# Scores for the maxima as three float32r products of split keys, one slot later, in a 32-batch perceiver kernel

## The reference

```
q = _split_heads(query @ Wq.T + bq)          # 64 rows, 16 heads of 16
k = _split_heads(bank @ Wk.T + bk)           # 1601 rows
v = _split_heads(bank @ Wv.T + bv)
scores = jnp.einsum('bhqd,bhkd->bhqk', q / score_scale, k)
attn = jax.nn.softmax(scores, axis=-1)
ctx = jnp.einsum('bhqk,bhkd->bhqd', attn, v)
```

## Time and profile before

| | before |
|---|---|
| time, median of 3 runs | 2134.21 us |
| lowest and highest run | 2132.24, 2140.06 us |
| span of the profiled execution | 2136.6 us |
| PE busy | 1977.4 us (93%) |
| DVE busy | 1327.4 us (62%) |
| ACT busy | 1050.5 us (49%) |
| POOL busy | 616.4 us (29%) |
| mean granted PE clock | 0.982 of 2.4 GHz |

### The profile page before, as it was taken

How to read it: one execution, slowest core, us unless ns; L and a number is a source line. 1 busy time by engine, 2 the same in 40 slices (tenths; PEclk the granted TensorE clock), 3 DMA queues, 4 the chain that set the end, 5 groups by cost and what they waited for, 6 DMA issues and landing times.

```text
span 2136.6 us, 72531 instructions
## 1 busy us (share of the span) xinstructions
PE 1977.4 (93%) x31780; PEld 1592.0 (75%) x31796; DVE 1327.4 (62%) x2500; ACT 1050.5 (49%) x1532; POOL 616.4 (29%) x998
## 2 busy tenths in 40 slices
PE   6789989999999999999999999999999998999987
PEld 4677777777877777787778777777777776777764
DVE  2656656856756666666666576675666666666644
ACT  3354445555465555455554544555545444444442
POOL 3223322323233232333323233342323222122201
PEclk7999999999999999999999999999999999999999
DMA  5433433343432333434333423343342321222122
GB/s 177 164 127 117 158 108 113 121 142 122 147 113 82 123 137 123 151 104 146 105 108 127 150 77 128 106 153 107 113 149 80 117 77 45 92 85 82 49 71 69
DMA packets 98358, 243.89 MB, mean 114 GB/s; under 512 B 12416, under 2 KB 18688, under 8 KB 98048
## 3 DMA queue, kind: packets, MB, share of 16 engines
q1 hardware_dynamic: 97456, 239.22, 32.7%
q10 hardware_dynamic: 592, 0.04, 0.0%
HBM read 235.94 MB, written 3.15 MB: 112 GB/s over the span
## 4 chain that ended last, share of the span: by engine, by line
PE 73%; DVE 13%; ACT 7%; issue 6%; POOL 1%; DMA 0%; ACTq 0%; DVEq 0%; POOLq 0%
PE M L798 11%; PE M L805 11%; PE SC L1016 9%; PE SC L1039 8%; PE O L1060 7%; PE X L855 5%; DVE mx L1607 4%; ACT probT L1262 4%; PE SC L1032 3%; PE M L855 3%; PE X L1126 2%; PE M L899 1%; PE X L1100 1%; PE M L860 1%; PE X L834 1%
## 5 line engine op out<-in xcount | busy, mean ns | idle before, releaser
L1607 DVE TENSOR_REDUCE mx<-SC 128x4 f32<-128x1600 f32 (+1 forms) x256 | 466.7, 1823 | 137.7 <-PE SC L1016 134.3
L1262 ACT ACTIVATE probT<-SC 128x2048 f32<-128x2048 f32 (+1 forms) x256 | 398.8, 1558 | 170.4 <-PE SC L1039 169.8
L647 POOL TENSOR_TENSOR rowsT<-raw,rowsT 128x384 fp32r<-128x384 f32 (+1 forms) x256 | 280.4, 1118 | 392.8 <-ACT rowsT L1316 392.7
L805 PE MATMUL M<-wvs,rowsT 128*128 128x256 f32 x2496 | 359.1, 293 | 4.1 <-issue 2.7
L798 PE MATMUL M<-rowsT,wks 128*128 128x400 f32 (+1 forms) x1536 | 343.8, 364 | 11.3 <-DVE V L1408 4.5
L1201 ACT ACTIVATE kT<-M,bk 128x400 f32<-128x400 f32 (+1 forms) x256 | 151.8, 594 | 385.5 <-PE M L798 385.1
L798 PEld LDWEIGHTS M<-rowsT,wks 128*128 128x128 f32 x1536 | 272.6, 191 | 86.4 <-issue 64.2
L1408 DVE TENSOR_TENSOR V<-M,bv 128x256 f32<-128x256 f32 (+1 forms) x448 | 159.5, 398 | 284.5 <-PE M L805 273.9
L805 PEld LDWEIGHTS M<-wvs,rowsT 128*128 128x128 f32 x2496 | 315.5, 192 | 24.5 <-issue 4.5
L1016 PE MATMUL SC<-kT,bdq 32*128 32x400 f32 (+1 forms) x2048 | 245.9, 548 | 27.1 <-ACT probT L1262 22.6
L1060 PEld LDWEIGHTS O<-probT,V 128*17 128x17 f32 x13312 | 195.1, 99 | 76.8 <-issue 72.2
(11 more groups left out here) (275 smaller groups left out, 2460.3 us busy)
## 6 DMA issues: line engine op xcount, KB each, us to landing
ring<-in_ws_dram SPq DMA_DIRECT2D x428, 256.0 KB, 4.5
raw<-in_ctx_dram SPq DMA_DIRECT2D x32, 1601.0 KB, 8.6
summed<-in_ctx_dram SPq DMA_DIRECT2D x60, 800.5 KB, 4.6
ring<-rounded_scratch SPq DMA_DIRECT2D x64, 256.0 KB, 5.9
out_dram<-x SPq DMA_DIRECT2D x16, 128.0 KB, 2.0
kT<-in_ctx_dram SPq DMA_DIRECT2D x2, 800.5 KB, 10.2
x<-in_x_dram SPq DMA_DIRECT2D x11, 128.0 KB, 2.1
rounded_scratch<-wround SPq DMA_DIRECT2D x8, 128.0 KB, 2.1
```

Of the source, the lines that this page charges most:

```text
L647: pool.tensor_tensor(rowsT[1][:, c, at], raw[:, c, at], rowsT[0][:, c, at], ALU.subtract).then_inc(low_ready, 1)
L805: mm = pe.matmul(bank[:, (t - 2 * a) * D:(t - 2 * a + 1) * D], rowsT[xp][:, cc, t * P:(t + 1) * P], wvs[wp][:, cc, :], start=(at == cc == ...
L1262: act.activation(probT[step % 3][0:w, :, 0:len(ts), :].rearrange("p j t q -> p j (t q)"), SC[0:w, :, 0:len(ts) * P], ACT.Exp)\
L1607: dve.tensor_reduce(mx[c][:, :, n], SC[:, :, 0:KCH[n][1]], AX.X, ALU.max).then_inc(max_used, 1)
```

## The change

From the second batch on (steps 8 to 255, 248 of them) the scores for the maxima are made from split operands. ACT copies a quarter of the finished keys, rounded to float32r, into `ks[..][0]` (`high_keys`, 400 or 402 columns, at the end of the slot two before that of the maxima); POOL subtracts that from the keys into `ks[..][1]` (`low_keys`, at the start of the next slot); the queries are split in the same way once a batch (`high_queries` in slot 0, `low_queries` in slot 2). PE makes twelve float32r matmuls in the place of four float32 ones: for each of three products (high by high, high query by rest of key, rest of query by high key) the four strips. The first batch keeps the old form. `LEAD` goes from 6 to 5, which puts each max block, the DVE reduction and `nmx` one slot later against the scores; the fills "max0" and "max1" stay where they are. `split_max` moves from the front of POOL's slot to behind `layer0`. Three warming blocks stand at the start where four did. The key drain writes an even number of columns.

```diff
-LEAD = 6
+LEAD = 5
-FIRST_WARM = (1, 2, 3, 4)
+FIRST_WARM = (1, 2, 3)
+SPLITS = 2
+def split_step(b, k, ahead):
+    s = STEPS * b + k + LEAD + ahead
+    return s if STEPS <= s < STEPS * B else None
+        ks = [sp.sb(f"ks{n}", [P, 2, KW], F32R) for n in range(SPLITS)]
+        qs = [sp.sb(f"qs{n}", [P, 2, C, 2 * S], F32R) for n in range(2)]
...
+                def low_queries(b):
+                    pool.wait_ge(q_high, b)
+                    pool.tensor_tensor(qs[b % 2][:, 1, :, :], bdq[b % 2].rearrange("p c e q -> p c (e q)"), qs[b % 2][:, 0, :, :], ALU.subtract)\
+                        .then_inc(q_low, 1)
+                def low_keys(s):
+                    mb, c, n, k0, w = chunk_of(s)
+                    pool.wait_ge(key_high, s - STEPS + 1)
+                    pool.tensor_tensor(ks[s % SPLITS][:, 1, 0:w], keys(mb, c)[:, k0:k0 + w], ks[s % SPLITS][:, 0, 0:w], ALU.subtract)\
+                        .then_inc(key_low, 1)
...
                 for b, k in SLOTS:
                     g = STEPS * b + k
+                    s = split_step(b, k, 1)
+                    if s is not None:
+                        low_keys(s)
                     if k == (2 if b == 1 else 0) and b >= 0:
                         block_queries(b + 1)
-                    if k == 2 and b >= -1:
-                        split_max(b, 1)
-                        if b < 0:
-                            block_queries(0)
-                    if k == 6 and b >= -1:
-                        split_max(b + 1, 0)
+                    if k == (3 if b == 1 else 2) and 0 <= b < B - 1:
+                        low_queries(b + 1)
+                    if (b, k) == (-1, 2):
+                        block_queries(0)
...
+                    if k == 2 and b >= -1:
+                        split_max(b, 1)
+                    if k == 6 and b >= -1:
+                        split_max(b + 1, 0)
...
+                    if mb:
+                        if s % STEPS == 0:
+                            pe.wait_ge(q_low, mb)
+                        pe.wait_ge(key_low, s - STEPS + 1)
+                        w = kn + kn % 2
+                        for at, (qp, kp) in enumerate(((0, 0), (0, 1), (1, 0))):
+                            for j in range(4):
+                                r = slice(32 * j, 32 * j + 32)
+                                mm = pe.matmul(SC[:, j, 0:w], qs[mb % 2][r, qp, c, :], ks[s % SPLITS][r, kp, 0:w],
+                                               start=(at == 0), stop=(at == 2), skip_group_check=True)
+                        mm.then_inc(max_filled, 1)
+                        return
...
+                def high_keys(s):
+                    mb, c, n, k0, w = chunk_of(s)
+                    wait_drained(act, (mb, "key", n, c))
+                    act.wait_ge(max_filled, s - SPLITS + 1)
+                    act.activation(ks[s % SPLITS][:, 0, 0:w], keys(mb, c)[:, k0:k0 + w], ACT.Copy).then_inc(key_high, 1)
...
+                    if k == (2 if b == 1 else 0) and 0 <= b < B - 1:
+                        high_queries(b + 1)
+                    s = split_step(b, k, 2)
+                    if s is not None:
+                        high_keys(s)
```

16 lines of the change are left out of this document (14 added, 2 removed).

## The result

| | before | after |
|---|---|---|
| time, median | 2133.49 us | 2200.15 us |
| ratio, 95% interval | | 1.0279, 1.0254 to 1.0305 |
| span of the profiled execution | 2136.6 us | 2198.6 us |
| mean granted PE clock | 0.982 | 0.962 |

A forecast was written before the change was run, and what follows sets the result against it. PE was taken as the bound, busy 1977.4 of 2136.6 us. Terms of -30 (max block), +30 (waits for the split), +17 (ACT) and -0.5 us (warming block) made +16.5 on 2134.2: about 2151 us, range 2106 to 2182.

The forecast's parts named there:

- ACT: Copies ahead of the exponentials delay PE: 14 us in 24 places, +17 us with the query copy; bounds 0 to +27.
- POOL: Key-rest and query-rest subtractions on POOL, made a slot before PE uses them: costed at nothing if less than a slot late.
- query copies: On ACT, ahead of slot 1: the query copy adds 0.4 us in some eight of the 24 places.
- The max block: On PE, twelve float32r matmuls take 0.76 us instead of 0.88: 0.12 us a step, -30 us over 248 steps.
- The rival of the weights: Max block: weights not loaded behind their own strip's matmuls, gain 3 instead of 30 us; about 2178 us, chance 0.11.
- the serial strips: Max block: float32r strips do not run side by side, 2.18 us instead of 0.88; +322 us, about 2470, chance 0.03.
- Two bounds: Max block: -40 us if strips stream at 0.42 ns a column; about 2470 us if strips do not run side by side.
- The waits for the split: PE ahead of L1088, slots 3 and 7: 20 waits of 1.04 us and 17 of 0.53, +30 us; bounds 0 to +64.
- The term for the key copies: ACT's 128 x 400 copy ahead of the exponentials holds up PE in 24 places by 0.59 us each: 14 us.
- POOL becomes late: Key rests 0.5 us late in a third of the steps, PE loses 41 us more; about 2192 us, chance 0.10.

The follow-up runs named there:

- e2: Kernel before, six steps ahead, with the twelve float32r products from key and query parts filled once; no splitting: 2113.00 us, ratio 0.9864.
- e14: Kernel before with e2's products, maxima five steps ahead and POOL's split at the back of its slot; no copies or rests: 2150.85 us, ratio 1.0061.
- e15: e14 plus POOL's subtraction and ACT's copy each slot, on buffers of their own, nobody waiting for the results: 2173.82 us, ratio 1.0149.
- e17: e15, with POOL's subtraction also waiting for ACT's copy of the slot before; PE waits for neither: 2181.44 us, ratio 1.0198.
- e11: e2 plus one ACT copy of 128x400 at the end of a slot that nobody waits for, nothing on POOL: 2117.95 us, ratio 0.9913.
- e7: Changed kernel without ACT's 248 key copies; high parts filled once, POOL subtracts as soon as the keys are there: 2170.67 us, ratio 1.0155.
- e6: Changed kernel without POOL's 248 key-rest subtractions; low part filled once, PE waits for ACT's copy instead: 2159.78 us, ratio 1.0107.
- e10: e2 plus one POOL subtraction of 128x400 a slot, on buffers of its own, that nobody waits for: 2123.65 us, ratio 0.9934.
- e3: Changed kernel with 1 to 10 idle matmuls in each of 40 places where PE waits: 2191.19 us, ratio 1.0225.
- e18: e17, with PE's max block also waiting for the subtraction of its step: 2194.76 us, ratio 1.0267.

## Why the prediction was wrong

Read as a ladder, each rung one of the runs above:

| step | ratio | us | forecast |
|---|---|---|---|
| products (e2) | 0.9864 | -29 | -30 |
| move of the maxima, one warming block less (e14) | 1.0061 | +42 | +30 - 0.5 |
| subtractions and copies run, unwaited (e15) | 1.0149 | +19 | +14 (ACT), 0 (POOL) |
| POOL waits for ACT's copy (e17) | 1.0198 | +10 | 0 |
| what is left (the change) | 1.0279 | +17 | +3 (query copies) |

Each rung is uncertain by some 10 us, so the 10 us of e17 are not clear of nothing.

*The max block* was right: 0.75 us measured for 0.76, and -29 us for -30. L798, which differs in shape alone, was the row to take. The Trainium skill (TensorE: Matmul & The Clock Gate, Part 3, "What overlaps and what doesn't") says that a weight load overlaps running matmuls only when it goes to another row group. The prediction's sum by that rule was a block of 0.87 us and a gain of 3 us; neither the block nor e2 agrees. The rival of the weights is refuted, and the serial strips with it. Two bounds were summed wrongly, without weight in the forecast: groups of 0.17 us give a block of 0.73 or 0.74 and a gain of 35 to 37 us, not 40, and serial strips give 2134.2 + 322 + 46.5, about 2503 us, not 2470.

*The waits for the split* were right in kind, place and count: 28.8 us in 33 places against 30 in 37. Their price in time was 33 us alone, with 30 inside the interval, and 42 with the short block, 32 to 52: there the forecast's 0.53 and 1.04 us a place were a little short.

*ACT.* The term for the key copies, 14 us, lies between the 10 us that they cost by running (e11) and the 26 us that go when they are taken out together with POOL's wait for them (e7). That the copies and the subtractions together cost 19 us unwaited at five steps (e15), near the 14 of the sum, is luck: the sum had them all with ACT. The forecast that the max block's wait would grow from 22.6 to 40 us failed: it is 24.8, in 64 places for 46. A part of that is that the new block starts 0.10 us behind the exponentials where the old one started 0.14 behind them.

*POOL* is the step that failed: "The rest of a key quarter is made a slot before PE uses it, some 7 us ahead, so I cost it at nothing; the cover is that POOL is less than a slot late." The condition held. In the changed kernel each of the 248 rests ends 3.6 us or more ahead of its max block, half of them 9.4 us or more, and still 37 us of the 60 go when the rests are left out (e6). The step asked only whether the result comes in time for PE. It left out that the subtraction holds up DVE's operations beside it, which by itself goes with 36 us more of DVE's busy time and 15 us of time at six steps (e10). The other 22 us are not traced to a mechanism. POOL's new wait for ACT's copy at the head of its in-order queue (583.5 us of standing) has at most the 10 us of e17 in its favour, which are not clear of the noise. The sentence on what is queued behind POOL's waits looked at the one for `nmx` only, and not at this one.

The rival "POOL becomes late" had the sign, and 2192 us, at a chance of 0.10. Its mechanism, rests that come late for the max block, is refuted: none does.

*The clock* had no term at all. PE ran 167 us at half rate for 77, which is at most 45 us of time if PE was at work in all of it. Undoing two thirds of the fall in e3 brought 12 us (2 to 22).

What stays open is the last rung, 17 us between e17 and the changed kernel. In the two profiled executions PE's waits are the same in all (199.9 and 201.5 us), and PE is busy 17 us longer (1973.5 and 1990.9) with nearly the same number of matmuls, at a clock of 0.970 and 0.962; so the rung shows as a lower clock there, and what lowers it is not shown. Several things differ: the subtractions are 0.14 us longer, the query parts are made (31 copies, 31 subtractions), ACT's copy waits 16.9 us for max blocks to free its buffer, and the wait ahead of the product behind the recurrence is 13.1 us for 9.1. No run takes out one of these alone. By the medians in place of the ratios this rung would be some 25 us.

## What to carry to other kernels

An operation added to an engine with half its time idle can cost time though its result is never late: ask which operations of another engine it will run beside, and what follows its wait in the in-order queue. To price such work before building all of it, run the operation with nobody waiting for it, then add the waits one at a time; and look in the trace whether an added wait is ever the last one, since a wait that is never late still took 0.11 us a place here. And ask first how exact the result has to be: the change that kept the maximum exact lost 60 us, and one rounded product with the old lead gains 3.3%.

## What the runs showed of the hardware

Float32r matmuls on four strips run side by side, and their weights are loaded while the matmuls of the group before run. L1056 of the changed kernel by stretch (length, busy time and how many started in it, granted clock, the DMAs' share and GB/s):

```profile
914.90:915.20 0.30, 0.21 (x4) 1.00 0.32 82
914.90:915.40 0.50, 0.41 (x8) 1.00 0.22 57
914.90:915.80 0.90, 0.81 (x12) 1.00 0.15 43
```

Four of the block have started by 915.20, eight by 915.40, and taking two of the three groups away shortens the block from 0.75 to 0.38 us, 0.19 a group: as much as one float32r matmul of that width on the whole array.

A DVE operation whose operands are all in SBUF is held up by a POOL subtraction that began before it: L1786 took 1.15 us where it takes 0.42 without the long subtraction beside it, and ended 0.29 us after POOL's. In all 16 places of the changed kernel's trace where it began inside a POOL operation of more than 0.5 us it took 1.13 to 1.24 us, and it ended 0.28 us after POOL's end. The Trainium skill (SBUF — State Buffer, "SBUF: two separate sides") says that DVE with two SBUF inputs and a GpSimd operation that reads SBUF contend for one pair of ports, and that the later of the two is held for the whole instruction of the other. This trace agrees for L1786, within the 0.14 us by which its 0.28 us behind POOL's end are less than its own 0.42. DVE's scan of the same shape (L1787) went from 0.69 to 1.09 us above, and in 20 of the 21 places where it began inside such a POOL operation it ended 0.55 us after POOL's end. It goes the other way too: of the 248 key rests, 38 took 0.06 us or more above their median of 1.05, and 37 of these began while DVE was at work on SBUF operands. Operations that read PSUM are not held: L1473 adds a bias to values in PSUM, and takes 0.41 us (median) with or without a long POOL operation beside it; here two of them beside a subtraction:

```profile
822.78 1.04 POOL L701 TENSOR_TENSOR ks<-kT,ks 128x400 fp32r<-128x400 f32 x1 [2.09 <-ACT ks L1370]
823.15 0.75 DVE L1473 TENSOR_TENSOR V<-M,bv 128x256 f32<-128x256 f32 x2 [0.39 <-PE M L840]
```

Seen over the kernel, 36 us more of DVE's time beside 248 subtractions went with 15 us of the kernel's.

One more semaphore that PE waits for ahead of a block, even one that was raised long before, moved the block from 0.14 to 0.26 us behind the exponentials (e17 and e18).

Filling waits with matmuls brought the mean clock from 0.9645 to 0.976 (means of four executions) and 12 of 60 us back, 2 to 22 with the intervals: a low granted clock in a profile is as much a mark of waits as a cause of time.
